# Expert outputs added into the residual rows by the scatter itself, and a last stage that only copies memory to memory

## What is computed

```
out = x + attention(xn)                      # 16 heads of 16, causal, RoPE
        + shared_ffn(xn)                     # silu(xn Wsg) * (xn Wsu) Wsd
        + sum_j score[n, j] * expert[idx[n, j]](xn[n])   # 32 experts, top 4 of each token
```

## Time and profile before

| | us |
|---|---|
| median of 3 runs (2672.46 to 2676.88) | 2676.68 |
| the profiled execution, its own time | 2683.8 |
| its span, first to last instruction | 2681.6 |
| stage A, up to the first instruction behind the barrier | 0 to 1936.4 |
| stage BC, up to the barrier at its end | 1936.4 to 2557.0 |
| stage D | 2557.0 to 2681.6 |

### The profile page before, as it was taken

How to read it: one execution, slowest core, us unless ns; L and a number is a source line. 1 busy time by engine, 2 the same in 40 slices (tenths; PEclk the granted TensorE clock), 3 DMA queues, 4 the chain that set the end, 5 groups by cost and what they waited for, 6 DMA issues and landing times. The chain is left out here.

```text
span 2681.6 us, 43680 instructions
## 1 busy us (share of the span) xinstructions
PE 1982.5 (74%) x11279; PEld 1203.6 (45%) x11280; DVE 1349.7 (50%) x3123; ACT 871.7 (33%) x1668; POOL 997.4 (37%) x993
## 2 busy tenths in 40 slices
PE   5778888778788778888777888861888888887700
PEld 2344443334444333443434444330477777776600
DVE  5645546364564545546454454630344444444467
ACT  1323233132322313223232323310255556555500
POOL 4523333432333433233442333446044444444500
PEclk8878888877887877888887887885799999999955
DMA  6052250505325051441505235052544444444389
GB/s 154 25 91 44 60 89 17 100 17 86 51 53 89 22 95 28 75 60 43 98 20 87 43 60 89 22 93 94 175 135 136 136 135 144 138 138 134 101 295 331
DMA packets 217833, 254.99 MB, mean 95 GB/s; under 512 B 74549, under 2 KB 166462, under 8 KB 217664
## 3 DMA queue, kind: packets, MB, share of 16 engines
q1 hardware_dynamic: 160128, 161.90, 28.9%
q0 software_dynamic: 35840, 71.63, 7.8%
q10 hardware_dynamic: 21824, 20.98, 2.5%
HBM read 112.54 MB, written 94.64 MB: 77 GB/s over the span
## 5 line engine op out<-in xcount | busy, mean ns | idle before, releaser
L715 DVE TENSOR_REDUCE neg<-ps_u 128x2 f32<-128x768 f32 (+3 forms) x384 | 392.7, 1044 | 365.9 <-PE ps_u L935 175.5
L494 POOL DMA_INDIRECT table<-entry,slot x256 | 253.8, 991 | 560.9 <-ACT xs L578 462.1
L1207 POOL DMA_INDIRECT y_dram<-yb_all,ent x288 | 283.5, 984 | 327.2 <-ACT yb_all L1163 233.0
L962 PE MATMUL ps_u<-q_st,k_st 50*128 50x512 f32 (+3 forms) x1024 | 205.1, 463 | 188.1 <-DMA q_st<-neg_t 107.4
L915 PE MATMUL ps_g<-we_gu 128*128 128x512 f32 x512 | 263.7, 647 | 60.1 <-DVE hid L702 43.9
L496 POOL DMA_INDIRECT values<-xs,slot x256 | 248.8, 972 | 83.3 <-issue 83.3
L600 ACT ACTIVATE we_d<-ps_u 128x1024 f32<-128x1024 f32 x160 | 163.5, 1023 | 345.0 <-PE ps_u L973 149.7
L931 PE MATMUL ps_u<-k_st,q_st 48*128 48x128 f32 (+3 forms) x1024 | 196.3, 421 | 74.7 <-DVE neg L715 26.2
L481 POOL TENSOR_TENSOR we_d<-we_d 128x512 f32<-128x512 f32 x64 | 81.3, 1270 | 440.8 <-DVE we_d L685 438.0
L962 PEld LDWEIGHTS ps_u<-q_st,k_st 50*128 50x128 f32 x1024 | 106.5, 239 | 290.0 <-issue 113.0
L600 ACT ACTIVATE probs<-ps_u 128x1024 f32<-128x1024 f32 x160 | 161.5, 1022 | 196.2 <-PE ps_u L973 167.4
(11 more groups left out here) (155 smaller groups left out, 3005.6 us busy)
## 6 DMA issues: line engine op xcount, KB each, us to landing
xg<-values SPq DMA_DIRECT2D x288, 128.0 KB
ys<-y_dram SPq DMA_DIRECT2D x64, 512.0 KB, 5.4
q_st<-we_gu SPq DMA_DIRECT2D x192, 128.0 KB
k_st<-we_gu SPq DMA_DIRECT2D x192, 128.0 KB
we_gu<-x SPq DMA_DIRECT2D x16, 512.0 KB
xres<-x SPq DMA_DIRECT2D x16, 512.0 KB
sum_dram<-osum SPq DMA_DIRECT2D x16, 512.0 KB
we_gu<-wgu_e ACTq DMA_DIRECT2D x16, 512.0 KB
```

The source lines that it names most:

```text
L494: pool.indirect_dma_start(table[:, :], bass.IndirectOffsetOnAxis(ap=slot[:, k:k + 1], axis=0), entry[:, k, :], None).then_inc(scattered, 16)
L715: nc.vector.tensor_reduce(neg[:, g % 2, i, :, k0:k0 + nk], ps[:, :, 0:nk * n].rearrange("p a (k n) -> p a k n", n=n), AX.X, ALU.max, negat ...
L962: nc.tensor.matmul(ps[:, a, lo:lo + n], k_st[rows, h, kt * P:(kt + 1) * P], q_st[rows, h, kt * P:SEQ], start=(lo == 0), stop=False, skip_g ...
L1207: pool.indirect_dma_start(y_dram[:, :], bass.IndirectOffsetOnAxis(ap=ent[k][:, 0:1], axis=0), yb[k][:, :], None, bounds_check=TOKENS * TOP ...
```

## The change

- Two DRAM tensors become one. `acc` holds the 8192 rows of the residual sum (stage A stores them there) and behind them `SPARE` = 2176 rows that belong to no token. `y_dram` and `sum_dram` are gone.
- The destination in a table entry is the token's own row. Blank entries get distinct rows of the spare part instead of an index out of bounds; these rows are written like the others. They are set to zero by one more DMA on SP's queue right behind the blanking of the table.
- The scatter of block n adds (`compute_op=ALU.add`): the DMA has to read the 128 rows of `acc`, add, and write them. Inside one block, and among the blocks of one expert, all rows differ. Blocks of two experts may hold the same token, so a new row vector `apart` (16 where the expert changes or the block is behind the last filled one, else 0) makes POOL wait for the three scatters before. POOL also waits in every case for the scatter of block n - 3 (`FLIGHT` = 3), so that at most three are in flight. Blocks 0 to 18 don't look at `apart` and wait for all of the three before them.
- `apart` is made by five more DVE instructions in the plan, and POOL reads one word of it before each block from 19 on.
- SP no longer loads `sums_in`.
- Stage D is 16 DMAs from `acc` to `out`, 512 KB each, eight on SP's queue and eight on ACT's, and no engine computes.

```diff
-            const(pool.iota(dest_f[:], pattern=[[P * TOPK, NT], [1, TOPK]], base=0, channel_multiplier=TOPK,
+            const(pool.iota(dest_f[:], pattern=[[P, NT], [0, TOPK]], base=0, channel_multiplier=1,
...
+                    sp.dma_start(acc[TOKENS:TOKENS + SPARE, :].rearrange("(k p) d -> p k d", p=P),
+                                 zeros[:].rearrange("p (o d) -> p o d", o=1).broadcast_to([P, SPARE // P, D])
+                                 ).then_inc(spare_set, 16)
...
-            def scatter(n, k, first):
+            def scatter(n, k):
+                static = isinstance(n, int) and n < NR + FLIGHT
+                if not static:
+                    other = pool.value_load(apart[0:1, bass.ds(n, 1)], min_val=0, max_val=16)
+                for back in range(1, FLIGHT + 1):
+                    if isinstance(n, int) and n < back:
+                        continue
+                    kb = (k - back) % NR
+                    past = (n - back - kb) * (16 // NR)
+                    pool.wait_ge(y_out[kb], past + 16 if static or back == FLIGHT else past + other)
                 pool.wait_ge(y_sb, n + 1)
                 hold(pool, passed)
-                pool.indirect_dma_start(y_dram[:, :], bass.IndirectOffsetOnAxis(ap=ent[k][:, 0:1], axis=0),
-                                        yb[k][:, :], None, bounds_check=TOKENS * TOPK - 1, oob_is_err=False
-                                        ).then_inc(y_out[k], 16)
+                pool.indirect_dma_start(acc[:, :], bass.IndirectOffsetOnAxis(ap=ent[k][:, 0:1], axis=0),
+                                        yb[k][:, :], None, compute_op=ALU.add).then_inc(y_out[k], 16)
...
-def phase_d(nc, sb_, sem, y_dram, sums, out):
+def phase_d(nc, sem, acc, out):
...
+        def runs(dram, k):
+            return dram[k * rows:(k + 1) * rows, :].rearrange("(a r) d -> a (r d)", r=8)
...
+            for k in range(PIECES):
+                sp.dma_start(runs(out, k), runs(acc, k)).then_inc(copied[0], 16)
+            sp.wait_ge(copied[0], 16 * PIECES)
```

More of the change, by code:

```diff
@@ L58 @@
 SKIP = 1 << 24
+SPARE = -(-(P + TABLE // P - 1) // P) * P
 EPS = 1e-5
@@ L825, in rank_c @@
                 back.link(b, nc.vector.tensor_copy(entry[:, :, 0], dest_f[:]))
-                back.link(b, nc.vector.tensor_scalar(dest_f[:], dest_f[:], float(SEQ * TOPK), None, ALU.add))
+                back.link(b, nc.vector.tensor_scalar(dest_f[:], dest_f[:], float(SEQ), None, ALU.add))
                 nc.vector.tensor_copy(slot[:], slotf[:]).then_inc(slots, 1)
@@ L1039, in _, with phase_bcd, phase_bc @@
                       "down": down, "oproj": oproj, "rank": rank})
[L1042 to L1053, removed]
+def phase_bcd(nc, sb_, sem, ident, iota_e, counts, we_gu, we_d, ps_g, ps_u, ps_av, values, acc, table, out):
+    phase_bc(nc, sb_, sem, ident, iota_e, counts, we_gu, we_d, ps_g, ps_u, ps_av, values, acc, table)
+    phase_d(nc, sem, acc, out)
+def phase_bc(nc, sb_, sem, ident, iota_e, counts, we_gu, we_d, ps_g, ps_u, ps_av, values, acc, table):
     stack = ExitStack()
@@ L1095, in phase_bc, with expert_loop @@
         BODY = NR
+        FLIGHT = 3
         LOOPS = (NBLOCK - 2 * NR) // BODY
         assert NBLOCK == 2 * NR + LOOPS * BODY
-        def expert_loop(eng, stage, once=None):
+        def expert_loop(eng, stage):
             for n in range(NR):
@@ L1133, in stage @@
                                  ).then_inc(block_in[k + q], 16)
[L1135 to L1142, removed]
+            expert_loop(sp, stage)
         @block.scalar
@@ L1356, in _ @@
                 stage(n, n % NR, False)
-def phase_d(nc, sb_, sem, y_dram, sums, out):
+def phase_d(nc, sem, acc, out):
     stack = ExitStack()
     with stack:
[L1362 to L1370, removed]
-        block = stack.enter_context(nc.Block())
[L1372 to L1379, removed]
+        PIECES = 8
+        rows = TOKENS // (2 * PIECES)
+        copied = [sem("copied_sp"), sem("copied_act")]
+        def runs(dram, k):
+            return dram[k * rows:(k + 1) * rows, :].rearrange("(a r) d -> a (r d)", r=8)
+        block = stack.enter_context(nc.Block())
@@ L1390, in _ @@
         @block.scalar
         def _(act):
[L1392 to L1409, removed]
-                    dve.wait_ge(stored[k], (n - k) * (16 // ND))
-                nc.vector.tensor_tensor(res[k][:], red[k][:, 0, :],
-                                        sums[:, bass.ds(n, 1), :].rearrange("p o d -> p (o d)"), ALU.add).then_inc(added, 1)
-            tiles(dve, add)
@@ L1417, in _rope_tables @@
+            for k in range(PIECES, 2 * PIECES):
+                act.dma_start(runs(out, k), runs(acc, k)).then_inc(copied[1], 16)
+            act.wait_ge(copied[1], 16 * PIECES)
 def _rope_tables():
```

48 lines of the change are left out of this document (28 added, 20 removed).

## The result

| | before | predicted | after |
|---|---|---|---|
| median, us | 2676.78 (4 runs, 2672.46 to 2677.56) | 2659 (2622 to 2780) | 2728.84 (4 runs, 2726.82 to 2731.10) |
| ratio | | 0.993 | 1.0198, 95% interval 1.018 to 1.0216 |
| profiled span, us | 2681.6 | | 2729.0 |

The kernel is slower by 2.0%; the forecast had the sign wrong. The time lies inside the range. The two profiled spans differ by 47.4 us, and that difference is taken apart here.

What follows compares the result with a forecast made beforehand. It took SP's issuing to bind stage BC and the DMA stage D. Terms -84.6 + 34.8 + 39.4 - 16 + 1.9 + 6.6 gave -17.9 us, so 2676.7 became 2659 us, range 2622 to 2780.

Steps and rivals of the forecast that it cites:

- blocks 19 to 271: Stage BC: scatter waits take 15.0 us an expert, covered by SP's issuing at 17.1 us; 0 us.
- r: What reading and adding cost on top of a plain chained scatter's 3.3 us step; taken as 1.0 us, step 4.3.
- rival 2: Stage BC: the adding scatter is slow enough to bind POOL; about +39 us, 2716 us at r = 2.0; chance 0.24.
- SP's slack of 9.5 us: Blocks 0 to 18: time SP's loads, 16 blocks later, can spare, taken off POOL's lag of 44.3 us.
- blocks 0 to 18: Start of stage BC: 18 chained steps of 4.3 us, 77.4 instead of 33.1; +34.8 us after SP's slack.
- the sums loads: Stage BC: 16 load issues leave SP, the supposed bound, at 1.0 us each; -16 us.
- the empty blocks: End of stage BC: 16 chained steps of 4.3 us, 68.8 instead of 29.4; +39.4 us.
- stage D: Copies replace the last stage's loads and sums: 40 us, from 28 to 53, instead of 124.6; -84.6 us.
- The zeroing: Stage A: 2.23 MB on SP's full queue ahead of the second sequence's load; +6.6 us.
- Rival 1: Adding scatters: only the bytes pass twice, r under 0.7; -42 us, 2635 us at r = 0.32; chance 0.14.
- rival 3: Adding scatters: an engine's rows go one after another; +285 us, 2962 us at r = 4; chance 0.14.
- Rival 4: Stage BC: POOL's register load, register instructions and waits bind at 2.0 us a block; +50 us, 2727 us; chance 0.06.

Runs made afterwards that it cites:

- the kernel with both edits: The changed kernel, but empty blocks don't scatter and blocks 1 to 18 also look at `apart`; 2610.73 us, ratio 0.9952 to the kernel before.

## Why the prediction was wrong

**The step that failed** is in blocks 19 to 271: "the next two follow at POOL's pace (1.4 us with the added instructions), the other 5.5 at a third of a step", 15.0 us an expert, and "So these waits are covered by SP's issuing: **0 us**". POOL's pace is 1.86, because the adding instruction itself takes 1.557 us in place of 0.983. The step at a change is 5.03 rather than 4.3. The same sum with these two gives 18.9 us an expert, over the 17.5 that before took for it, and the cover is gone: 30 times 1.4 are the 41 us. I had priced the DMA that the scatter starts (r) with bounds on both sides, and the instruction that starts it with the row of another form of it. The doubt stood in rival 2 ("may cost POOL more to issue too, which no row shows") without a bound or a price of its own. The quantity that the prediction called decisive did not turn the sign: r came out at 1.35, inside its own 0.7 to 1.5, and with it the prediction's own sum would still have ended near -6 us. The stated range holds the time only because it was drawn out for rivals 2 and 4.

**What follows from it.** With POOL as the bound, its lag in blocks 0 to 18 is not shared with SP's slack of 9.5 us, and the -16 for the sums loads falls away. The reckoning by the numbers of the ledger, measured less predicted: blocks 0 to 18 +16, the middle +41, the sums loads +16, the empty blocks +6, stage D -12, the start -1, the drain -1. Together +65, from -17.9 to +47.3.

**Sizes.** r came out at 1.35 (predicted 1.0, the sign to turn at 1.5) and is itself a sum of 0.60 on POOL and 0.75 in the DMA. The mean step, 4.70 in the empty blocks and 4.68 in blocks 0 to 18 against 4.3, is all of the 6 us there and 7 of the 16 here; the other 9.5 are the slack. Stage D took 28.1 us, the lower bound of 28 to 53: its time is that of each copied byte counted once at 337 GB/s, plus 3 us. The zeroing moved the barrier by 6.3 us on two chips (6.6 predicted), and DVE's wait became 14.21 (15 predicted), 5.7 more than before.

By the Trainium skill ("DMA: Bandwidth & Descriptors", "Latency and other measured facts") the estimate for stage D was 42 us. It took 28.1, 8.39 MB at 299 GB/s with first issue and landing in it. The page's 207 to 214 GB/s are of tiles whose rows lie 512 KiB or more apart; for these contiguous copies the measurement decides, and the figure doesn't carry over. By the halved rate of adding transfers that the Trainium skill states ("Collectives: The Full Stack", "The bandwidth ceiling") the estimate for r was 0.32; the DMA's share alone was 0.75 here.

**The rivals.** Rival 1 is refuted by the step of 4.6, rival 3 as well. Rival 4 gave the right signature, a constant distance near 2.0 inside an expert, and 2727 us, the nearest number of all, but by luck, for its cause is wrong: the register load and the waits don't widen the gap ahead of an adding scatter, which is 0.30 us with and without them (ahead of a plain one the least gap grew to 0.33 to 0.37). Rival 2 named the right bound, POOL, and two places: the waits for block n - 3, which the run with six in flight excludes, and those at each change of expert, which do count (without them the kernel with both edits gained 82 us).

## What to carry to other kernels

When an operation moves into a DMA, price two things: what the transfer takes, and what the issuing engine takes to describe it; a form that no row shows needs a bound for each. When slack is spent, add up all that draws on it: here the longer instruction alone and the waits alone each stayed within the old pace (the instruction alone cost 20 us against a plain one, which the dropped sums loads paid for), and only together they broke the cover. And ask whether the bound that lends the slack is one of instructions or one of the chip at hand: the pace of the kernel with both edits was equal on two chips (2.220 and 2.222 us) while the old one's was 2.08 on one and 1.65 on another.

## What the hardware showed beyond that

- An adding indexed scatter of 128 rows takes POOL 1.551 to 1.557 us by the median of each profile, a plain one 0.958 to 0.983, and an adding one of 64 rows 1.40.
- Chained scatters of 128 rows step at 3.23 us plain and 4.58 adding.
- 16 copies of 512 KB from memory to memory, contiguous, need 28 to 29 us in all.
- POOL's drain at the end of stage BC took 4.55 to 4.88 us after adding scatters of 128 rows and 7.57 to 7.99 after plain ones, but 7.21 after adding ones of 64 rows: the addition alone doesn't decide it, and the cause is open.
- One chip ran the unchanged kernel in 2076 and 2087 us, the others in 2623 to 2677 by their medians; 481 of the 597 us between its profile and the first lie in stage A, at a granted clock of 0.94 against 0.80.
